# Twelve expert tiles set into the drain of a time-mix pipeline

## The chip, the cores and the metric

The kernel runs on one core of a Trainium2 chip. The metric is the device time of one execution in microseconds (us), lower is better; where several executions were timed, the median is given.

## What is computed

`x` has 64 sequences of 32 tokens with 256 channels (2048 tokens), `ctx` 64 sequences of 257. All arithmetic is float32. Three blocks follow each other, each with its residual:

```
x = x + xattn(layernorm(x), ctx)          # cross attention with LoRA projections
x = x + attn(layernorm(x))                # RWKV: time-mix, then a mixture of 8 experts
x = x + ffn(layernorm(x))                 # shared GEGLU + one of 8 GEGLU experts
```

The middle block is the one that matters here:

```
x  = x + (r * wkv) @ Wo                   # time-mix: a scan over the 32 tokens of a sequence
ei = ln(x);  exx = shift(ei)              # the row of the token before, zero for the first
probs = softmax(ei @ router_w);  two experts a token, weights vals / vals.sum
xk = ei * mk[e] + exx * (1 - mk[e]);  xr = the same with mr[e]
k_e = square(relu(xk @ eWk[e]));  kv = k_e @ eWv[e]        # 256 -> 512 -> 256
moe = sum over the two experts of  w * sigmoid(xr @ eWr[e]) * kv
```

## The kernel before

The 2048 tokens are G = 16 chunks of 128. Five engines run instruction streams of their own (SyncE `sp` only issues DMAs), held together by counting semaphores; within an engine the order of the program is the order of execution.

**Attention and time-mix** (`mix_sync`, `mix_pool`, `mix_tensor`, `mix_scalar`, `mix_vector`) are one software pipeline of STEPS = 25 steps. At step s attention works on chunks s to s-2, the time-mix on chunks s-3 to s-6 (LAG = 3), the router on s-7 and s-8; at s-9 the chunk's tokens are written into the table `tab_e` with two indirect DMAs (`list_tokens`, L475), by expert and rank. From step 16 on no new chunk enters: the pipeline drains. At step s GpSimd also makes the normed rows of chunk s-7 (`normed`, L460 and L462, four buffers `ei`), and SyncE stores them into `rows_e` (`store_normed`): one store of 128 rows (L326) and four of 31 rows, shifted by one token, for the four sequences of a chunk (L329). A buffer of `ei` is written again only when the store four chunks back has landed.

At step 18 SyncE issues the expert weights: `eWk` (4 MB, L354), `eWr` (2 MB, L356), `eWv` (4 MB, L358) and the small `Wg` (L360), ahead of that step's `store_normed`. They all go through SyncE's one queue. They lie in `arena_a`, over the keys and values of the attention, and so need it finished (`dv_x1`).

After step 24 TensorE makes the totals per expert (`totals`, L689) and VectorE the `tile_map` (L1017 to L1035): for each of NT1 = 39 tiles of 128 tokens its expert (`expert1`) and its place in `tab_e` (`place1`).

**The expert loop** (`moe_*`) then runs over 39 tiles in MSTEPS = 41 steps. SyncE loads the 128 token numbers of a tile (`pick`, L1131, nine tiles ahead). GpSimd copies the expert's mixing factors (`mu_e`, L1171) and gathers the pairs of rows by an indirect DMA (L1172, three tiles ahead); before the first it waits for every store of normed rows and for the tile map. At step m TensorE transposes tile m (L1192), does the hidden matmuls (L1200) and the receptance (L1207) of tile m-1 and the down projection (L1215) of tile m-2. ScalarE copies the transposed half and the expert's weights (L1231, L1234), then relu and sigmoid (L1238, L1241). VectorE mixes (L1271, L1278), squares (L1285) and gates (L1290); SyncE stores the result to `rows_y` (L1146). Buffers have NM = 3 slots. The steps are written out for the first 6 and the last 2, and run as a hardware loop of three steps a trip between them (`sweep`). At step 4 VectorE computes `slot1`, the row of `rows_y` of each token's two results (`rows_of`, L1253 to L1262). The combine, the second router and the GEGLU stages follow.

## Time and profile before

| | |
|---|---|
| median of 3 runs | 1026.53 us (1026.32 to 1027.2) |
| profiled execution | 1027.74 us, span of its instructions 1026.0 us |
| TensorE busy | 892.7 us (87%) |
| VectorE, ScalarE, GpSimd busy | 420.8 (41%), 293.2 (29%), 309.4 us (30%) |
| granted TensorE clock, mean | 0.942 of full |
| DMA | 163.55 MB, mean 159 GB/s |

The profile's times are microseconds from the first instruction. PE is TensorE's matmuls, PEld its weight loads (they overlap), DVE VectorE, ACT ScalarE, POOL GpSimd, SP SyncE; a q behind the engine marks a DMA that it issues. L460 is line 460 of the kernel before. A timeline row gives start, duration, engine, line, operation, what is written and from what, how many, and in brackets the idle time before it and what ended that. Names are those of the buffers in memory: nearly everything of the mix and the expert loop is called `arena_a`, `arena_b` or `bank`.

### The profile page before, as it was taken

The page shows a single profiled execution, that of the slowest core. Times are in us where ns is not written, and L with a number is a line of the kernel's source. Part 1 is how long each engine was busy: PE and PEld are TensorE (multiplying, and loading weights), DVE is VectorE, ACT ScalarE, POOL GpSimd, SP SyncE. Part 2 cuts the span into 40 slices and gives each one's busy share as a digit, 9 for nine tenths or more (in the row PEclk, how much of TensorE's full clock was granted, in tenths as well). Part 3 has the DMA queues.
Part 4 walks back from the last instruction along what each step waited for, and adds up shares of the span by engine and source line. Part 5 has one row for each costly group of instructions (what it writes and reads, how often), then busy time and mean ns, then how long its engine had stood idle before and what let it go on. Part 6 is the DMA issues. An engine that isn't in the chain of part 4 may idle for free. (4 is left out here: it accounts for less than half of the span.)

```text
span 1026.0 us, 20031 instructions
## 1 busy us (share of the span) xinstructions
PE 892.7 (87%) x6725; PEld 810.2 (79%) x6726; DVE 420.8 (41%) x1145; ACT 293.2 (29%) x666; POOL 309.4 (30%) x545
## 2 busy tenths in 40 slices
PE   5799999999730299999994999996899999999994
PEld 4577787887630299999994999995799999999993
DVE  2346776767841165555552333336211111111113
ACT  1345555554420155455441111110011111111110
POOL 1832555655652333322213222221210010110005
PEclk8899999999965599999997999998999999999998
DMA  9844555520791232263222111110598988899715
GB/s 345 268 170 155 182 128 165 192 73 22 197 220 41 57 88 78 78 202 89 77 61 62 31 35 43 31 31 26 196 321 331 312 310 327 296 324 328 261 57 164
DMA packets 100354, 163.55 MB, mean 159 GB/s; under 512 B 12440, under 2 KB 78616, under 8 KB 98104
## 3 DMA queue, kind: packets, MB, share of 16 engines
q1 hardware_dynamic: 86960, 120.93, 36.3%
q0 software_dynamic: 7552, 19.56, 7.3%
q10 hardware_dynamic: 5776, 22.22, 5.5%
q8 instruction: 37, 0.61, 0.3%
q14 instruction: 29, 0.24, 0.1%
HBM read 146.08 MB, written 16.60 MB: 159 GB/s over the span
## 5 line engine op out<-in xcount | busy, mean ns | idle before, releaser
L1524 PEld LDWEIGHTS bank<-zT_f,we 128*128 128x128 f32 x1472 | 167.8, 192 | 2.1 <-ACT zT_f L1812 0.7
L1524 PE MATMUL bank<-zT_f,we 128*128 128x128 f32 x1472 | 168.3, 275 | 0.5 <-ACT zT_f L1812 0.5
L1541 DVE TENSOR_TENSOR hT_f<-bank,act_g 128x512 f32<-128x512 f32 x78 | 53.9, 692 | 228.4 <-PE bank L1524 208.7
L1533 ACT ACTIVATE act_g<-bank 128x512 f32<-128x512 f32 x78 | 46.6, 597 | 321.5 <-PE bank L1524 318.0
L1524 PE MATMUL bank<-zT_c,a_x 128*128 128x128 f32 x1024 | 121.6, 281 | 0.3 <-PEq L1354 0.3
L1524 PEld LDWEIGHTS bank<-zT_c,a_x 128*128 128x128 f32 x1024 | 119.4, 197 | 0.8 <-issue 0.7
L572 PE MATMUL bank<-arena_b,mixed_w 128*128 128x128 f32 x768 | 91.5, 276 | 0.0
L572 PEld LDWEIGHTS bank<-arena_b,mixed_w 128*128 128x128 f32 x768 | 89.2, 192 | 1.0 <-issue 0.4
L1548 PE MATMUL bank<-we,hT_f 128*128 128x256 f32 x368 | 83.2, 379 | 0.0
L1200 PE MATMUL bank<-arena_b 128*128 128x128 f32 x624 | 77.8, 279 | 0.3 <-DVE hT L1285 0.2
L1200 PEld LDWEIGHTS bank<-arena_b 128*128 128x128 f32 x624 | 74.4, 195 | 0.9 <-DVE arena_b L1278 0.5
L1548 PEld LDWEIGHTS bank<-we,hT_f 128*128 128x128 f32 x368 | 68.1, 190 | 8.3
L1215 PE MATMUL bank<-arena_a,hT 128*128 x312 | 73.8, 379 | 0.7 <-DVE arena_b L1290 0.7
L1215 PEld LDWEIGHTS bank<-arena_a,hT 128*128 128x128 f32 x312 | 59.2, 190 | 9.1 <-issue 1.1
L1548 PE MATMUL bank<-mixed_w,hT_f 128*128 128x256 f32 x256 | 59.9, 388 | 4.1 <-issue 3.4
L1753 POOL COPY pick_f<-table 128x1 uint32 (+1 forms) x23 | 4.2, 184 | 186.5 <-PE bank L1774 159.1
L1548 PEld LDWEIGHTS bank<-mixed_w,hT_f 128*128 128x128 f32 x256 | 48.6, 195 | 11.0 <-issue 3.8
L1192 PE MATMUL bank<-ident,arena_b 128*128 128x128 f32 x156 | 24.4, 281 | 31.5 <-DMA arena_b<-rows_e,pick 30.4
L1192 PEld LDWEIGHTS bank<-ident,arena_b 128*128 128x128 f32 x156 | 19.9, 144 | 35.6 <-issue 30.4
L1278 DVE SCALAR_TENSOR_TENSOR arena_b<-arena_b,mu_e 128x128 f32<-128x128 f32 x156 | 45.4, 353 | 6.3 <-issue 6.0
L1231 ACT ACTIVATE arena_b<-bank 128x256 f32<-128x256 f32 x39 | 15.0, 384 | 115.2 <-PE bank L1192 115.1
L1234 ACT ACTIVATE arena_b<-arena_a 128x1024 f32 x39 | 41.2, 1057 | 13.1 <-issue 13.1
(249 smaller groups left out, 1323.6 us busy)
## 6 DMA issues: line engine op xcount, KB each, us to landing
we<-in_W_dram SPq DMA_DIRECT2D x69, 1024.0 KB, 7.2
arena_a<-in_ctx_n_dram ACTq DMA_DIRECT2D x16, 1152.0 KB
arena_a<-in_ctx_t_dram SPq DMA_DIRECT2D x16, 1028.0 KB, 9.8
rows_y<-arena_b SPq DMA_DIRECT2D x39, 128.0 KB, 2.0
arena_a<-in_eWk_dram SPq DMA_DIRECT2D x1, 4096.0 KB, 21.2
arena_a<-in_eWv_dram SPq DMA_DIRECT2D x1, 4096.0 KB, 38.4
rows_f<-yr ACTq DMA_DIRECT2D x23, 128.0 KB, 6.1
rows_e<-arena_b SPq DMA_DIRECT2D x16, 128.0 KB
```

Of the source, the lines that this page charges most:

```text
L572: last = nc.tensor.matmul(of_seq(bank[:, m * P:(m + 1) * P]), mixed_w[:, i, k, h, m * P:(m + 1) * P], xn[n % 2][:, k, :, 1 - h:1 - h + S], ...
L1192: last = nc.tensor.transpose(bA[:, q * P:(q + 1) * P], pair[:, a.slot, q * P:(q + 1) * P], ident[:])
L1200: last = nc.tensor.matmul(bHh[:, f * P:(f + 1) * P], wk_e[:, b.slot, k * FK + f * P:k * FK + (f + 1) * P], xk[:, b.slot, k * P:(k + 1) * P ...
L1215: last = nc.tensor.matmul(bY[:, 0:D], hT[:, d.slot, f * P:(f + 1) * P], ewv_sb[:, e, f * D:(f + 1) * D], start=f == 0, stop=f == FKC - 1)
L1231: nc.scalar.activation(prevT[:, a.slot], bA[:, 0:KD * P], ACT.Copy).then_inc(m_ap, 1)
L1234: nc.scalar.activation(wk_e[:, a.slot], ewk_sb[:, e], ACT.Copy).then_inc(m_awk, 1)
L1278: last = nc.vector.scalar_tensor_tensor(o[:, a.slot, h], diffT[:, a.slot, h], mu_e[:, a.slot, i, k:k + 1], prevT[:, a.slot, h], ALU.mult, ...
L1524: last = nc.tensor.matmul(bank[half][:, f * P:(f + 1) * P], w12[:, i, k, col0:col0 + P], zT[:, k], start=k == 0, stop=k == KD - 1)
L1533: nc.scalar.activation(act_g[:, half], bU[half][:], ACT.Gelu).then_inc(self.ac_g, 1)
L1541: nc.vector.tensor_tensor(hT[:, parity, half * HH:(half + 1) * HH].rearrange("p f t -> p (f t)"), bG[half][:], act_g[:, half], ALU.mult).t ...
L1548: last = nc.tensor.matmul(bY[parity][:, 0:D], hT[:, parity, f], w3[:, f], start=f == 0, stop=f == HC - 1)
L1753: nc.gpsimd.tensor_copy(pick[:, s.slot], table2[:, bass.ds(s.n, 1)]).then_inc(picked, 1)
```

## The change

- **Two phases of tiles.** The first CUT = 10 chunks are routed on their own. When chunk 10 is ranked (step 18), TensorE also makes the totals of the ten chunks and VectorE a first tile map (`tile_map_a`) of the *full* tiles only; TA = 12 of them are taken (`taken_a`: how many of each expert). The second map, after step 24, covers the other 27 tiles. `slot1` needs to know for each token which phase it fell into (`row_numbers`, now about eighteen VectorE operations, at expert step 12).
- **The expert steps are set into the drain.** Expert step m runs at the end of mix step s = 20 + m on each engine; the steps 0 to 4 share mix steps 20 to 24, the rest follow. At the end of step 19 SyncE issues the picks of the twelve tiles and GpSimd gathers the first three, which waits for these picks.
- **Weights in five pieces**: at step 16 `eWk` of experts 0 to 5 and `eWr` of 0 to 5, at 17 `eWk` 6 to 7 and `eWv` 0 to 4, at 18 `eWv` 5 to 7 and `eWr` 6 to 7, each *behind* that step's `store_normed`. `eWr` moves into `xz`, whose first chunks are free early; `w_T` and `early` move to the end of `arena_a`.
- **Unrolled, fewer buffers, other queue**: all 42 expert steps are written out. Weight copy, mixed rows, hidden and sigmoid have two slots instead of three. ScalarE issues the stores to `rows_y`, a step later. The expert loop uses the banks bS, bWV, bQR and bVV.

The core of the diff:

```diff
+        CUT = 10
+        TA = 12
+        MOE_AT = G + LAG + 1
+        MSTEPS = NT1 + 3
...
+        def moe_pick(sp, tiles):
+            for n in tiles:
+                mapped(sp, n)
+                if n == 0:
+                    sp.wait_ge(po_tab_a, 2 * 16 * CUT)
+                if n == TA:
+                    sp.wait_ge(po_tab, 2 * 16 * (G - CUT))
+                at = sp.value_load(place1[0:1, n:n + 1], min_val=0, max_val=T_ROWS // P - 1)
+                sp.dma_start(pick[:, n], tab_e[bass.ds(at * P, P), :]).then_inc(picked_by(n)[0], 16)
+
+        def moe_pool(pool):
+            def gather(n):
+                mapped(pool, n)
+                if n in (0, TA):
+                    for i in range(EI):
+                        pool.wait_ge(ei_out[i], OUT_PER * len(range(i, G if n else CUT, EI)))
...
+                e = pool.value_load(expert1[0:1, n:n + 1], min_val=0, max_val=E - 1)
+                need(pool, m_dx, n - NM + 1)
+                pool.wait_ge(*picked_by(n))
+                nc.gpsimd.tensor_copy(mu_e[:, n % NM], cm_mu[:, :, e]).then_inc(m_mu, 1)
+                rows = rows_e[0:CUT * P, :] if n < TA else rows_e[:, :]
...
+            def step(m):
+                if m < NT1:
+                    copies(m)
+                if 0 <= m - 1 < NT1:
+                    units(m - 1)
+                if 0 <= m - 3 < NT1:
+                    store(m - 3)
...
+                if m == TA:
+                    row_numbers()
...
+                if g is not None:
+                    store_normed(g)
+                if s == G:
+                    sp.wait_ge(pe_s, G)
+                    load_k(0, 6, 2)
+                    load_r(0, 6, 0)
+                if s == G + 1:
+                    sp.wait_ge(dv_o, G)
+                    load_k(6, E, 3)
+                    load_v(0, 5, 3)
                 if s == G + 2:
                     sp.wait_ge(dv_x1, G)
-                    sp.dma_start(ewk_sb.rearrange("p e (k f) -> p e k f", k=KD),
-                                 eWk.rearrange("e (k p) f -> p e k f", p=P)).then_inc(ld_moe[0], 16)
...
+                    load_v(5, E, 4)
+                    load_r(6, E, 1)
+                if s == MOE_AT - 1:
+                    moe_pick(sp, range(TA))
+            sp.dma_start(r2_w[:], Wg.rearrange("(k p) e -> p k e", p=P)).then_inc(ld_s, 16)
+            moe_pick(sp, range(TA, NT1))
...
+                if s == MOE_AT - 1:
+                    for n in range(NM):
+                        gather(n)
+                if s >= MOE_AT:
+                    moe(s - MOE_AT)
+            for m in range(STEPS - MOE_AT, MSTEPS):
+                moe(m)
...
+                if h == CUT:
+                    tile_map_a()
```

## Rows read from the trace of the kernel before

**Rows 1.** Busy us of each engine by stretch; granted clock, DMA share, GB/s
```profile
300.00:320.00 20.00, 0.89 (x6) 0.66 (x5) 1.40 (x9) 1.46 (x2) 3.89 (x7) 0.50 0.47 110
...
360.00:380.00 20.00, 20.00 (x136) 18.56 (x135) 11.92 (x35) 9.99 (x19) 7.65 (x12) 1.00 0.29 82
```

**Rows 2.** Waits from 250 to 360 us: total, times, longest
```profile
POOL arena_b L460 <- DMA rows_e<-arena_b: 15.8, 1, 15.8
```

**Rows 3.** Timeline of SyncE's DMA issues, 247 to 350 us
```profile
247.81 1.53 SPq L329 DMA_DIRECT2D rows_e<-arena_b  x4
...
262.19 0.41 SPq L354 DMA_DIRECT2D arena_a<-in_eWk_dram  x1
...
283.31 17.88 SPq L360 DMA_DIRECT2D r_w<-in_Wg_dram  x1
...
333.81 4.29 SPq L329 DMA_DIRECT2D rows_e<-arena_b  x4
339.21 10.32 SPq L1131 DMA_DIRECT2D pick<-tab_e  x10
```

**Rows 4.** DMA: GB/s in 40 slices (300 to 345 us); KB, us to landing
```profile
GB/s 244 264 210 122 88 169 191 170 66 134 24 25 24 24 134 24 25 24 8 12 123 2 9 8 4 0 14 24 25 24 133 25 24 25 24 25 24 25 24 9
...
pick<-tab_e SPq DMA_DIRECT2D x10, 0.5 KB, 2.7
r_w<-in_Wg_dram SPq DMA_DIRECT2D x1, 8.0 KB, 26.8
```

**Rows 5.** Timeline, 295 to 350 us: a drain step, the tile map, the first gathers
```profile
295.84 0.22 POOL L447 TENSOR_SCALAR rs<-mv 128x1 f32<-128x1 f32 x1
...
297.13 0.60 ACT L797 ACTIVATE arena_b<-a_x,rs 128x256 f32<-128x256 f32 x1 [1.75 <-POOL rs L451]
...
299.49 1.02 PE L623 MATMUL bank<-r_wg,arena_b 128*128 128x8 f32 x4
...
319.85 0.29 DVE L1017 TENSOR_TENSOR arena_b<-bank,tile_lo 128x128 f32<-128x128 f32 x1 [1.95 <-PE bank L689]
...
323.24 0.20 DVE L1035 TENSOR_TENSOR place<-te_f,tb_f 128x39 int32<-128x39 f32 x1
...
345.82 0.19 POOL L1171 COPY mu_e<-late 128x4 f32 x1 [23.68 <-issue]
...
349.27 0.98 POOL L1172 DMA_INDIRECT arena_b<-rows_e,pick  x1 [0.16 <-issue]
```

**Rows 6.** Timeline of the expert loop, 353 to 544 us
```profile
353.53 3.66 PE L1200 MATMUL bank<-arena_b 128*128 128x128 f32 x16
...
367.96 0.60 PE L1192 MATMUL bank<-ident,arena_b 128*128 128x128 f32 x4
...
372.77 0.60 PE L1192 MATMUL bank<-ident,arena_b 128*128 128x128 f32 x4
...
512.87 1.95 PE L1200 MATMUL bank<-arena_b 128*128 128x128 f32 x16
...
514.15 1.14 DVE L1278 SCALAR_TENSOR_TENSOR arena_b<-arena_b,mu_e 128x128 f32<-128x128 f32 x4 [0.16 <-issue]
...
517.69 1.95 PE L1200 MATMUL bank<-arena_b 128*128 128x128 f32 x16
...
543.80 0.43 DVE L1290 TENSOR_TENSOR arena_b<-bank,arena_b 128x256 f32<-128x256 f32 x1 [2.29 <-PE bank L1215]
```

**Rows 7.** Timeline of VectorE at expert step 4: first and last of five
```profile
368.50 0.16 DVE L1253 TENSOR_TENSOR moved<-t_end,n_tiles 128x8 f32<-128x8 f32 x1
...
369.98 0.22 DVE L1262 SCALAR_TENSOR_TENSOR slot<-moved_k,listed 128x32 uint32<-128x32 f32 x1
```

**Rows 8.** As rows 1, in stretches of 4 us
```profile
284.00:288.00 4.00, 1.92 (x13) 1.24 (x11) 3.60 (x12) 0.90 (x3) 2.15 (x3) 1.00 1.29 216
288.00:292.00 4.00, 1.37 (x3) 1.18 (x4) 3.10 (x11) 0.27 (x1) 3.45 (x8) 0.58 0.80 232
...
356.00:360.00 4.00, 3.80 (x27) 3.44 (x26) 2.18 (x7) 2.21 (x4) 2.02 (x4) 0.88 0.42 120
```

More of the change, by code:

```diff
@@ L210, in perceiver_block @@
         in_a = Carve(arena_a, FLOATS_A)
-        w_T = in_a.take(4, KD, D)
+        kT = [in_a.take(BG, KD, KW) for _ in range(N3)]
+        ctx_sb = in_a.take(N3, BG * TC * D + D)
         early = in_a.take(EARLY)
@@ L214, in perceiver_block @@
         bv_b, bo_b = early[:, 4:4 + D], early[:, 4 + D:4 + 2 * D]
-        ctx_sb = in_a.take(N3, BG * TC * D + D)
-        kT = [in_a.take(BG, KD, KW) for _ in range(N3)]
         hn, v_own, o_nat = (in_a.take(2, D) for _ in range(3))
@@ new lines, in moe_tensor, with turned, hidden, receptance @@
+        def moe_tensor(pe):
+            def turned(n):
+                pe.wait_ge(m_got[n % NM], n // NM * 16 + 16)
+                if n == 0:
+                    pe.wait_ge(ac_exp, G)
+                need(pe, m_dd, n)
+                for q in range(2 * KD):
+                    last = nc.tensor.transpose(bMT[:, q * P:(q + 1) * P], pair[:, n % NM, q * P:(q + 1) * P], ident[:])
+                last.then_inc(m_pa, 1)
+            def hidden(n):
+                pe.wait_ge(m_dx, n + 1)
+                pe.wait_ge(m_awk, n + 1)
+                if n == 0:
+                    pe.wait_ge(ac_er, G)
+                need(pe, m_dsq, n)
+                for f in range(FKC):
+                    for k in range(KD):
+                        last = nc.tensor.matmul(bMH[:, f * P:(f + 1) * P],
+                                                wk_e[:, n % 2, k * FK + f * P:k * FK + (f + 1) * P],
+                                                xk[:, n % 2, k * P:(k + 1) * P], start=k == 0, stop=k == KD - 1)
+                last.then_inc(m_ph, 1)
+            def receptance(n):
+                mapped(pe, n)
+                e = pe.value_load(expert1[0:1, n:n + 1], min_val=0, max_val=E - 1)
+                if n == 0:
+                    pe.wait_ge(dv_x1, G)
+                    pe.wait_ge(dv_v, G)
+                    pe.wait_ge(ld_moe[0], 16)
+                    pe.wait_ge(ld_moe[1], 16)
+                need(pe, m_asig, n)
+                for k in range(KD):
+                    last = nc.tensor.matmul(bMR[:, 0:D], xr[:, n % 2, k * P:(k + 1) * P],
+                                            ewr_sb[:, e, k * D:(k + 1) * D], start=k == 0, stop=k == KD - 1)
+                last.then_inc(m_pr, 1)
+            def down(n):
+                e = pe.value_load(expert1[0:1, n:n + 1], min_val=0, max_val=E - 1)
+                if n == 0:
+                    pe.wait_ge(dv_ev, G)
+                    pe.wait_ge(ld_moe[3], 16)
+                    pe.wait_ge(ld_moe[4], 16)
+                pe.wait_ge(m_dsq, n + 1)
+                need(pe, m_dy, n)
+                for f in range(FKC):
+                    last = nc.tensor.matmul(bMY[:, 0:D], hT[:, n % 2, f * P:(f + 1) * P],
+                                            ewv_sb[:, e, f * D:(f + 1) * D], start=f == 0, stop=f == FKC - 1)
+                last.then_inc(m_py, 1)
+            def step(m):
+                if m < NT1:
+                    turned(m)
+                if 0 <= m - 1 < NT1:
+                    hidden(m - 1)
+                    receptance(m - 1)
+                if 0 <= m - 2 < NT1:
+                    down(m - 2)
+            return step
@@ L730, in mix_tensor @@
                     router(g)
-            totals()
+                if s == STEPS - 1:
+                    totals()
+                if s >= MOE_AT:
+                    moe(s - MOE_AT)
+            for m in range(STEPS - MOE_AT, MSTEPS):
+                moe(m)
         def mix_scalar(act):
@@ L878, in mix_scalar @@
                     load_values(s + 2)
+                if s >= MOE_AT:
+                    moe(s - MOE_AT)
+            for m in range(STEPS - MOE_AT, MSTEPS):
+                moe(m)
         def mix_vector(dve):
@@ L1292, in perceiver_block @@
-        assert NT1 % NM == 0
+                if s == STEPS - 1:
+                    tile_map()
+                if s >= MOE_AT:
+                    moe(s - MOE_AT)
+            for m in range(STEPS - MOE_AT, MSTEPS):
+                moe(m)
         with nc.Block() as block:
```

430 lines of the change are left out of this document (232 added, 198 removed).

## The prediction, made before the change was run

> **What bounds the kernel now.** I read the table of 20 us stretches first. TensorE works 0.9 of the 20 us from 300 to 320, at the lower clock, and all 20 from 360 on [rows 1]; the hole begins near 288 and ends when the first gathered tile is there, near 350 [rows 8, 5]. It lies between the time-mix and the expert loop, and it is the only thing this change can fill. The list of waits of that stretch names a part: GpSimd waits 15.8 us for a store of normed rows [rows 2]. The queue of SyncE tells why. The three weight loads go out at 262.2 us, the queue is held until 283.31 + 17.88 = 301.2, and then the stores of chunks 11 to 15 fill it until 338.1; the first pick of a tile's tokens is issued at 339.2 [rows 3]. The small Wg load, queued behind the weights, lands at 283.31 + 26.8 = 310.1 us [rows 3, 4]; I take that as the end of the weights too. From then on it isn't bandwidth: the bandwidth row shows 24 GB/s between short peaks, which are the 31-row stores one after another (31 KB at 24 GB/s is 1.3 us) [rows 4].
>
> Inside the expert loop TensorE sets the pace: a tile follows a tile every 4.81 us with all 20 of 20 us busy [rows 1], and the chain transposes, ScalarE copy, VectorE mix ends 2.4 us before its matmuls begin (515.29 against 517.69) [rows 6]. So the loop's 39 tiles cost the same TensorE time after the change; what can change is when tile 5 begins (372.77 us now [rows 6]) and what interrupts the rest.
>
> **Sum, part one: when the first tokens are there.** The weights may go out behind the store of chunk 9, which is issued by 249.3 us, instead of at 262.2 [rows 3]: 12.9 us earlier. They took 47.9 us (262.2 to 310.1). Alone that gives 297 us. But the stores of chunks 10 and 11 are now inside this stream and that of chunk 12 ahead of the picks. Each is one 128-row store and four of 31 rows, 4.29 us of queue for the four [rows 3]; at 1.3 us each to move, and 0.8 for the large one, I take 6 us. Does such a store lengthen the stream or run beside it? Not shown by any row, so I bound it: nothing (297 us) or all of it, 2 x 6 (309 us). The row that is nearest is the 24 GB/s: under the weights the sixteen engines moved 216 to 232 GB/s together, 14 each [rows 8], so 24 is what a single one does alone, and the four stores follow each other as on one and the same engine. That engine's share of the weights then comes last, and a load is complete only with it. I take 309. Chunk 12's store, 6 us, makes it 315; the first pick, 2 us to land [rows 4], 317.
>
> The Trainium skill (DMA: Bandwidth & Descriptors, section on why a DMA increments its semaphore by 16) says that a copy uses the largest number of engines up to 16 that divides its slowest dimension, and the lowest-numbered ones, so 31 rows go to a single engine, always the same. It speaks against this change, and by it the stream ends at 309, not at 297. The rate of [rows 4] agrees with one engine; that it is always the same one no row shows.
>
> GpSimd now waits for these picks at the end of step 19, ahead of its share of steps 20 to 24. This is the wait that the change adds, and it replaces the 15.8 us at step 22 [rows 2]. Queued behind it are the reciprocal deviations, numerators, normed rows, counts and token lists of the last chunks; ScalarE, TensorE and VectorE wait for these. Three gathers take 345.82 to 350.25, 4.4 us [rows 5]. GpSimd is free for step 20 at about 317 + 4.4 = 321 us (bound below 297 + 2 + 4.4 = 303.5).
>
> **Part two: five drain steps with expert steps 0 to 4 in them.** Hand schedule from t0 = 321, durations of [rows 5, 6]; TensorE is at half clock at first. Step 20: three small GpSimd operations 1.3 (295.84 to 297.13), then normalise, transpose, copy, router 3.4 (297.13 to 299.49 + 1.02), transposes of tile 0 1.1, mix to t0 + 8.3. Step 21: GpSimd issues a gather behind that mix, 1.6, then 1.3 + 3.4 again, to 14.7; transposes 1.1, hidden at half clock 3.5, receptance 1.7, to 21.2. Step 22: ScalarE does the sigmoid first, then the same chain at full clock 2.7, then a whole tile of TensorE work 4.8 and the gate, 29.7. Step 23: four small VectorE operations and the ranks 1.5, 4.8 of TensorE and the gate 0.5, 36.6. Step 24: the tile map, 319.85 to 323.44 now with two operations more, 3.7; the difference 0.45 and then mixing to 42. TensorE could transpose tile 5 at 41.1 and is set back 0.4 by the mix: t0 + 41.5. So tile 5 begins at 321 + 41.5 = 362.5 us instead of 372.8: 10.3 us gained.
>
> The rest of the change, by its place: the first tile map (at VectorE's step 18) is some 13 small operations with drains, 3 us against the 3.6 of the present one; it delays GpSimd's step 19, which waits for the picks anyway: nothing, 3 us if that wait were gone. The extra totals matmul and its waits: nothing. Two buffers instead of three for mixed rows, hidden and weight copies: each is reused when the matmuls two tiles back are done, a whole step earlier than needed by the 4.81 us rhythm: nothing. Stores of y on ScalarE's queue, one a tile: a pick's issue is about 1 us of SyncE [rows 3], and a store's can't be dearer by its kind; ScalarE is busy 10 of 20 us in the loop [rows 1]: nothing. The 27 later picks: each about 1.03 us of SyncE (10.32 for ten [rows 3]), 28 us from the tile map at about 361; tile 12 is gathered four steps later and needs only the first; nothing. Shared weights: loaded at step 27 of the expert loop, 362 + 22 x 4.8 = 468 us, well before the loop ends.
>
> The row numbers at step 12 grow from five VectorE operations, 1.7 us [rows 7], to about eighteen with drains, 6 us. VectorE has 0.4 us idle there and the mix has the 2.4 us above: TensorE waits 6 - 0.4 - 2.4 = about 3 us, once (0 to 5). Unrolling: steps 4 and 5 are written out before too and lie 4.81 us apart (367.96, 372.77); inside the loop it is 4.82 (512.87, 517.69) [rows 6]: nothing. The Trainium skill (Runtime: NRT & Kernel Launch, Instruction fetch mechanics) holds that a taken branch can stall the fetch of instructions, which would make the unrolled loop faster; the equal distances show no such stall here.
>
> **Sum.** 10.3 - 3 = 7.3 us less. The profiled execution took 1027.7 us (span 1026.0), 1.2 above the median of 1026.5. 1027.7 - 7.3 = 1020.4 for it, **1019 us** as a median.
>
> **Rivals.**
> 1. *The small stores run beside the weights.* Then t0 is 303.5 and all else follows: 17.5 us more are gained, 1002 us. For it: the stores of chunks 10 and 11 are 0.3 MB of the stream's 10.8 MB. Against it: the 24 GB/s, and GpSimd's 15.8 us for a store that was queued behind weights [rows 2, 4].
> 2. *TensorE stays at 1.2 GHz.* The granted clock fell to 1.2 GHz within 288 to 292 us, after TensorE had been busy 1.9 of 4 us, and came back to 2.4 within 356 to 360 [rows 8], some 3 to 4 us after unbroken work had begun at 353.5 [rows 6]. I let it come back in step 22. If the gaps of the drain hold it down through steps 22 to 24, the 4.8 us of expert work are 9.6 in three steps: +14.4, and 1019 + 14 = 1033 us, slower than before. It decides from about two such steps on.
> 3. *It overlaps nothing.* The picks land so late (5 to 8 us later than I say, a slower stream, or the store of chunk 12 held longer) that the drain plus five tiles ends where the drain, the stores, the picks and five tiles ended before: t0 = 329 gives 1026 to 1027 us, no change.
>
> **Chances.** My forecast, with its errors of the store price, the clock by one step (+5) and the row numbers, 1012 to 1024: 0.54. Rival 1, whole or in part, 1000 to 1011: 0.22. Rival 3: 0.10. Rival 2 or another slower course: 0.14. A measurement of this kernel can tell about 0.2% (2 us) from no change. Faster 0.76, same 0.10, slower 0.14. The range takes in rival 1's bound and rival 3 and leaves out most of rival 2: 1001 to 1028.
>
> **What would show it.** Right: the first weight load at about 249 us; the first pick landing near 317 and GpSimd idle some 30 us before its first copy of mixing factors; TensorE's hole from about 288 to 320 only; tile 5's transposes near 362; one gap of TensorE of 3 us at step 12; 4.81 us a tile elsewhere; the last gate near 537 instead of 543.8. Wrong: the first pick near 300; half clock beyond the drain; gaps of TensorE in the steady steps (double buffers, fetch of instructions, ScalarE's stores); or GpSimd still waiting for a store at step 22.

## The result, and the profile after

The changed kernel takes 1014.99 us in the median of four executions (1010.54 to 1017.74), the kernel before on the same chip 1026.57 us (1026.32 to 1027.2). The ratio is 0.988, with a 95% interval of 0.985 to 0.992. The profiled execution took 1014.11 us with a span of 1012.3 us, 13.7 us less than the span before. The forecast was 1019 us with a range of 1001 to 1028. One execution of a later variant, the one with six picks on ScalarE's queue, ran at a mean granted clock of 0.82 instead of 0.95 and took 1094 us; the figures below leave it out.

The two stretches of 20 us that answer to [rows 1] show that there is still a hole between the time-mix and the expert loop. From 300 to 320 us TensorE works 4.9 us now and worked 0.9 before; in stretches of 4 us it does nothing at all from 288 to 312 us, and before it worked 0.4 us in all from 304 to 348. The columns are the same as there.

```profile
300.00:320.00 20.00, 4.89 (x18) 3.85 (x18) 1.50 (x6) 3.56 (x6) 8.93 (x15) 0.50 0.23 55
360.00:380.00 20.00, 20.00 (x134) 18.46 (x133) 10.72 (x28) 9.71 (x16) 4.75 (x9) 1.00 0.35 87
```

The list of waits from 250 to 360 us names the new cause. In place of the 15.8 us of [rows 2], GpSimd stands 24.6 us at the first copy of mixing factors, for a pick, and TensorE waits with it:

```profile
PE bank L842 <- ACT arena_b L1098: 35.3, 4, 28.3
...
POOL mu_e L358 <- DMA pick<-tab_e: 24.6, 1, 24.6
```

SyncE's queue, which answers to [rows 3], has the weights (L585, L589, L594) and the stores of normed rows (L579 the 128 rows, L582 the four times 31) one behind the other:

```profile
248.73 0.40 SPq L585 DMA_DIRECT2D arena_a<-in_eWk_dram  x1
...
259.52 6.14 SPq L579 DMA_DIRECT2D rows_e<-arena_b  x1
265.70 5.90 SPq L582 DMA_DIRECT2D rows_e<-arena_b  x4
...
291.15 3.85 SPq L594 DMA_DIRECT2D xz<-in_eWr_dram  x1
295.05 1.27 SPq L579 DMA_DIRECT2D rows_e<-arena_b  x1
296.36 5.00 SPq L582 DMA_DIRECT2D rows_e<-arena_b  x4
302.46 7.04 SPq L344 DMA_DIRECT2D pick<-tab_e  x7
```

The bandwidth from 250 to 310 us, in 40 slices of 1.5 us, answers to [rows 4]. The last piece of the weights lands 11.1 us after its issue, at 302.2 us. Three times the rate falls: to 24, 31 and 8 GB/s from 271 to 275.5 us, to 59, 42 and 40 from 287.5 to 292, and to 24 from 299.5 us for some eight us, each time behind one of the three groups of 31-row stores in the queue. In the last 2.7 us before the last piece of the weights lands nothing but that 24 GB/s moves.

```profile
GB/s 150 53 166 285 408 408 388 350 149 108 205 238 268 113 24 31 8 216 350 356 374 358 345 340 152 59 42 40 245 380 378 348 138 23 23 25 24 24 8 0
...
xz<-in_eWr_dram SPq DMA_DIRECT2D x1, 512.0 KB, 11.1
```

The timelines of GpSimd, TensorE and VectorE give the dates that the sum was built on: the first copy of mixing factors, GpSimd free for step 20, the transposes of tile 0, those of tile 5, and the last gate, the counterpart of 543.80 us in [rows 6].

```profile
308.13 0.18 POOL L358 COPY mu_e<-late 128x4 f32 x1 [24.62 <-DMA pick<-tab_e]
...
312.65 0.23 POOL L728 TENSOR_SCALAR rs<-mv 128x1 f32<-128x1 f32 x1
```

```profile
317.18 1.09 PE L397 MATMUL bank<-ident,arena_a 128*128 128x128 f32 x4
...
354.58 0.63 PE L397 MATMUL bank<-ident,arena_a 128*128 128x128 f32 x4
```

```profile
530.40 0.42 DVE L552 TENSOR_TENSOR arena_a<-bank,sig 128x256 f32<-128x256 f32 x1 [2.29 <-PE bank L436]
```

### The profile page after: what moved, and what is told of

The parts are those of the page before. It is cut to its first block and busy times, and to the rows that moved or that the text cites. A ratio compares the mean times of both kernels' runs of the same rounds, so it can differ in the third digit from the quotient of the medians.

```text
span 1012.3 us, 19824 instructions
## 1 busy us (share of the span) xinstructions
PE 898.9 (89%) x6726; PEld 815.5 (81%) x6726; DVE 424.4 (42%) x1173; ACT 294.3 (29%) x665; POOL 308.9 (31%) x547
## 5 line engine op out<-in xcount | busy, mean ns | idle before, releaser
L863 PE MATMUL bank<-arena_b,mixed_w 128*128 128x128 f32 x768 | 94.2, 281 | 0.0
L863 PEld LDWEIGHTS bank<-arena_b,mixed_w 128*128 128x128 f32 x768 | 91.9, 197 | 1.1 <-issue 0.4
L408 PE MATMUL bank<-arena_b,arena_a 128*128 128x128 f32 x624 | 79.1, 282 | 2.6 <-DVE hT L546 2.6
L408 PEld LDWEIGHTS bank<-arena_b,arena_a 128*128 128x128 f32 x624 | 75.8, 198 | 3.0 <-DVE arena_b L538 3.0
L1721 PEld LDWEIGHTS bank<-mixed_w,hT_f 128*128 128x128 f32 x256 | 49.7, 200 | 13.2 <-DVE hT_f L1714 6.5
L358 POOL COPY mu_e<-late 128x4 f32 x39 | 7.3, 187 | 126.1 <-DVE arena_b L538 101.4
L464 ACT ACTIVATE arena_a<-arena_a 128x1024 f32 x39 | 41.3, 1059 | 10.3 <-issue 10.3
L360 POOL DMA_INDIRECT arena_a<-rows_e,pick x39 | 38.3, 983 | 18.1 <-issue 18.1
L423 PE MATMUL bank<-xz,arena_b 128*128 x156 | 40.7, 384 | 0.0
```

Source lines behind the costliest of these rows:

```text
L360: nc.gpsimd.indirect_dma_start(out=pair[:, n % NM], out_offset=None, in_=rows, in_offset=bass.IndirectOffsetOnAxis(ap=pick[:, n], axis=0)) ...
L408: last = nc.tensor.matmul(bMH[:, f * P:(f + 1) * P], wk_e[:, n % 2, k * FK + f * P:k * FK + (f + 1) * P], xk[:, n % 2, k * P:(k + 1) * P], ...
L423: last = nc.tensor.matmul(bMR[:, 0:D], xr[:, n % 2, k * P:(k + 1) * P], ewr_sb[:, e, k * D:(k + 1) * D], start=k == 0, stop=k == KD - 1)
L464: nc.scalar.activation(wk_e[:, n % 2], ewk_sb[:, e], ACT.Copy).then_inc(m_awk, 1)
L863: last = nc.tensor.matmul(of_seq(bank[:, m * P:(m + 1) * P]), mixed_w[:, i, k, h, m * P:(m + 1) * P], xn[n % 2][:, k, :, 1 - h:1 - h + S], ...
L1721: last = nc.tensor.matmul(bY[parity][:, 0:D], hT[:, parity, f], w3[:, f], start=f == 0, stop=f == HC - 1)
```

## The experiments

Except for the changed kernel run again, which is the same to the letter, and the kernel before with split stores, every experiment carries one small difference beside its own: the fourth weight semaphore counts two loads in the changed kernel, and the experiments wait for both (`wait_ge(ld_moe[3], 32)`). No run takes that difference by itself. Times are medians; each is compared with the kernel before on the same chip (1027.7 to 1029.1 us in the four groups), and the ratio with its interval is what can be compared across groups.

| kernel | median, us | ratio, 95% | tile 5 transposes | last gate |
|---|---|---|---|---|
| changed kernel again | 1018.39 | 0.989 (0.987 to 0.992) | 355.4 | 534.0 |
| + split stores | 1008.67 | 0.982 (0.980 to 0.984) | 346.6 | 522.4 |
| + 3 picks on ScalarE's queue | 1005.82 | 0.978 (0.976 to 0.981) | 344.7 | 522.2 |
| + no expert step in the drain | 1020.28 | 0.993 (0.990 to 0.995) | 362.4 | 536.7 |
| + row numbers in three parts | 1011.67 | 0.983 (0.980 to 0.986) | 355.9 | 528.5 |
| kernel before + split stores | 1016.45 | 0.988 (0.985 to 0.991) | 359.2 | 530.3 |
| + 6 picks on ScalarE's queue | 999.28 | 0.973 (0.969 to 0.978) | 337.3 | 513.2 |
| all three: split, 6 picks, rows | 1000.12 | 0.972 (0.969 to 0.975) | 342.7 | 515.3 |
| 6 picks, rows | 994.59 | 0.969 (0.966 to 0.972) | 336.9 | 509.5 |
| all three, nothing in the drain | 996.76 | 0.969 (0.967 to 0.972) | 341.9 | 513.0 |
| 6 picks, rows, filler, too long | 997.30 | 0.970 (0.968 to 0.972) | 343.2 | 515.8 |
| 6 picks, rows, filler, fitted | 990.49 | 0.965 (0.963 to 0.967) | 333.5 | 506.1 |

The row of six picks has the median of three executions. The last two columns come from the profiled execution of each. Executions also differ ahead of the part that matters: the first weight load goes out at 246.9 to 250.3 us in the profiles of the variants with whole stores, which are the same up to there. So up to some 3 us of a difference between two rows of these columns can be that.

### The changed kernel again

> The changed kernel once more, on the same chip as the three variants beside it. Theory: span near 1012 us; the first pick lands near 308 us and GpSimd is free for mix step 20 near 312.6, because the picks lie behind the weights and the store of chunk 12 on SyncE's queue. If its time moves by some us from execution to execution (1010.5 to 1017.7 so far), the profile should show it in that landing or in the drain, not in the steady expert steps of 4.81 us.

It took 1018.39 us (1014.15 to 1019.02), as before within the spread. Its profile holds a find. Tile 5 comes 0.8 us later than in the first profile, but the last gate 3.6 us later. The timeline of TensorE shows where: after the pause at the row numbers (L397 waits 1.55 us, L408 1.29 us) the eight hidden matmuls (x16, since each float32 matmul is recorded twice) take 3.75 us.

```profile
401.99 0.63 PE L397 MATMUL bank<-ident,arena_a 128*128 128x128 f32 x4 [1.55 <-DVE arena_b L531]
403.90 3.75 PE L408 MATMUL bank<-arena_b,arena_a 128*128 128x128 f32 x16 [1.29 <-DVE hT L546]
...
411.17 0.60 PE L397 MATMUL bank<-ident,arena_a 128*128 128x128 f32 x4
```

In the first profile the same step ran with the same pause, but its matmuls took their 2.02 us:

```profile
401.17 0.63 PE L397 MATMUL bank<-ident,arena_a 128*128 128x128 f32 x4 [1.55 <-DVE arena_b L531]
403.08 2.02 PE L408 MATMUL bank<-arena_b,arena_a 128*128 128x128 f32 x16 [1.28 <-DVE hT L546]
...
407.53 0.60 PE L397 MATMUL bank<-ident,arena_a 128*128 128x128 f32 x4
```

The granted clock of the second look confirms it. From 404 to 408 us it was 0.50, that is 1.2 of the 2.4 GHz, right behind a stretch in which TensorE had been busy 1.16 of 4 us:

```profile
400.00:404.00 4.00, 1.16 (x8) 0.58 (x6) 3.51 (x12) 1.08 (x2) 0.19 (x2) 0.86 0.01 2
404.00:408.00 4.00, 4.00 (x18) 3.91 (x19) 2.31 (x6) 0.67 (x2) 2.66 (x4) 0.50 0.23 70
```

In the first profile the same 4 us behind the row numbers held as little work, 1.17 us, and the clock stayed:

```profile
399.20:403.20 4.00, 1.17 (x7) 0.59 (x7) 3.53 (x13) 1.10 (x2) 0.22 (x2) 1.00 0.00 1
```

With the lower clock the step took 9.18 us instead of 6.36. A pause of 3.3 us can cost another 2.8 us of clock, and whether it does differs between executions of one and the same kernel.

### Split stores in the changed kernel

```diff
-  OUT_PER = 16 * (1 + BG)
+  OUT_PER = 16 * (1 + 2 * BG)
...
-  sp.dma_start(rows_e[r + 1:r + S, 0:D], ei[j*S:j*S + S - 1, n % EI]).then_inc(ei_out[n % EI], 16)
+  for lo, hi in ((0, 16), (16, S - 1)):
+      sp.dma_start(rows_e[r + 1 + lo:r + 1 + hi, 0:D],
+                   ei[j*S + lo:j*S + hi, n % EI]).then_inc(ei_out[n % EI], 16)
```

> One change to the changed kernel: each store of 31 shifted rows is issued as 16 rows and 15 rows, for all chunks; nothing else (this and the other variants also wait for both loads on the fourth weight semaphore). Theory A (the 31-row stores all use one DMA engine, lengthen the weight stream from 47.9 to 53.5 us and hold the picks by another 5 to 6 us): the weights land near 297 instead of 302, the first pick near 299.5 instead of 308.1, the whole is about 8 us faster than the changed kernel, 1005 to 1008 us. Theory B (small stores cost a fixed time each, whatever engines they use): eight small stores a chunk instead of four, first pick at 308 or later, 1015 or more.

1008.67 us, 9.7 less than the changed kernel. The first weight load went out at 250.80 us, 2.1 us later, because eight issues take longer than four (3.59 us against 1.53). All weights had landed at 285.01 + 12.9 = 297.9 us. That is a stream of 47.1 us, as long as the 47.9 of the kernel before, against 302.2 - 248.7 = 53.5 with whole stores. The bandwidth over the same 60 us (250 to 310) no longer stays at 24 GB/s anywhere. The stream with the stores of chunk 12 in it ends near 298 us, falling from full rate to nothing without a stretch at 24 (368, 299, 103 GB/s, then 3), and the 189 behind it are the gathers:

```profile
GB/s 36 89 233 273 365 408 391 367 225 172 167 189 266 205 35 250 175 338 382 327 267 340 329 166 31 78 132 235 340 368 299 103 3 0 1 189 189 153 1 1
```

GpSimd's wait for the pick fell from 24.6 to 16.8 us (first copy at 300.12 instead of 308.13). So four 31-row stores move at 24 GB/s and lengthen the stream and the way to the picks; the same rows as 16 and 15 show no such stretch. That 24 GB/s is one engine of sixteen can be read twice. The DMA share, the mean over the sixteen engines, is 0.08 where only these stores run, and one of sixteen is 0.06; and sixteen together reach 408 GB/s in the row above, 25.5 each.

```profile
300.00:304.00 4.00, 0.00 (x0) 0.00 (x0) 0.00 (x0) 0.00 (x0) 0.00 (x0) 0.50 0.08 24
```

That line is the changed kernel's. The Trainium skill (DMA: Bandwidth & Descriptors, section on why a DMA increments its semaphore by 16) gives the rule from which I had taken this: the largest number up to 16 that divides the slowest dimension is one for 31 rows and 16 or 15 for the halves. These runs agree with it; that it is always the same engine they don't show.

### Split stores in the kernel before

The same edit at L329 and of `OUT_PER`, and nothing of the change.

> The kernel before, with each store of 31 rows made as one of 16 and one of 15 rows, and nothing else: what the engine imbalance cost before the change. Theory (each 31-row store is moved by one DMA engine alone, 1.3 us each, and the stores of chunks 11 to 15 follow each other that way from 301 to 338 us, with the picks behind): GpSimd's wait of 15.8 us for a store shrinks to some 8 us, the last store leaves the queue at 320 to 325 us, bounded by the issue of 45 descriptors at 0.42 us behind the weights, the picks go at 323 instead of 339, and tile 5 begins 12 to 17 us earlier: 1010 to 1015 us. That would be as much as the whole change brings. Rival (the cost lies in the number of stores or in their completions one by one): the tail stays until 335 or later, since there are nearly twice as many stores, and the time stays within 4 us or rises.

1016.45 us (1015.0 to 1017.89): the ratio, 0.988, is that of the whole change. The expected 1010 to 1015 was a little too good. In the queue of SyncE the last chunks follow each other every 4.0 us, nine issues at 0.4 us each, where those of the kernel before went out at 301.2, 309.4, 314.5, 320.1 and 332.6, 5 to 12 us apart:

```profile
305.52 4.79 SPq L330 DMA_DIRECT2D rows_e<-arena_b  x8
...
322.89 3.57 SPq L330 DMA_DIRECT2D rows_e<-arena_b  x8
329.52 10.71 SPq L1133 DMA_DIRECT2D pick<-tab_e  x10
```

GpSimd's wait for a buffer shrank only from 15.8 to 13.2 us, not to 8: the queue issued the stores of that buffer only from 305 to 310, behind the weights. The picks go at 329.5 instead of 339.2 us, the first copy of mixing factors is at 332.6 instead of 345.8, and tile 5 at 359.2 instead of 372.8. An edit of four lines thus takes 13.6 us out of the same hole into which the change puts its two phases of tiles. On top of split stores the change still brings 0.988 to 0.982, 6 to 7 us.

### Three picks on ScalarE's queue

```diff
+  if s == MOE_AT - 1:
+      moe_pick(act, range(NM))          # in mix_scalar, the same step
...
-  moe_pick(sp, range(TA))
+  moe_pick(sp, range(NM, TA))
```

On either queue the first picks also wait for the first tile map and for the token lists of ten chunks.

> One change to the changed kernel: the picks of the first three tiles are issued by ScalarE on its own queue at the end of its step 19; the other nine stay where they are. Theory A (the wait that the change added, GpSimd for picks behind weights and stores, sets the end of the drain): the picks land near 289 us, GpSimd is free near 293 instead of 312.6, everything behind it moves by 19 us less what TensorE then waits for weights (they land at 302, needed for the receptance of tile 0 near 307, so little): about 996 us, 994 to 1000. Theory B (the wait is cover only: weights, clock or gathers are late next): the gain is 8 us or less, 1006 or more, with TensorE waiting for a load or the gather.

1005.82 us, 12.6 less than the changed kernel, not 19. The first copy of mixing factors comes at 292.97, 15 us earlier. But at the fourth tile GpSimd waits again, 9.3 us, since that tile's pick still stands behind weights and stores in SyncE's queue:

```profile
292.97 0.18 POOL L359 COPY mu_e<-late 128x4 f32 x1 [9.21 <-DMA pick<-tab_e]
...
312.92 0.18 POOL L359 COPY mu_e<-late 128x4 f32 x1 [9.30 <-DMA pick<-tab_e]
```

I had priced the first wait and not looked at who waits next in the same queue. This run is also the second with a lower clock behind the row numbers (1.7 us).

### Nothing in the drain

```diff
-  MOE_AT = G + LAG + 1
+  MOE_AT = STEPS
```

> One constant of the changed kernel: the expert steps start after mix step 24 instead of at step 20, so no expert step is set into the drain; the first twelve tiles, their early table and the early weights stay. Theory A (the overlap itself brings nothing, since GpSimd's wait stops the drain; what gains is that the tables and weights are early): the drain runs through without the 24.6 us wait and ends near 310 us, but the picks now lie behind the stores of chunks 13 to 15, near 324; transposes of tile 0 near 328, of tile 5 near 351, against 356 effectively in the changed kernel: 1009 to 1012 us, 2 to 6 us faster than the changed one. Theory B (setting the steps into the drain is what gains): tile 5 near 372 as in the kernel before, 1025 us.

1020.28 us, by the median 2 us slower than the changed kernel again, though the intervals overlap (0.990 to 0.995 against 0.987 to 0.992), with the tile map of ten chunks, early weights and all else kept. The miss is in the picks. The drain no longer waits for them, so the stores of chunks 13 to 15 get into the queue first (to 329.0 us) and the picks go at 330.1:

```profile
304.06 13.70 SPq L582 DMA_DIRECT2D rows_e<-arena_b  x4
...
324.73 4.29 SPq L582 DMA_DIRECT2D rows_e<-arena_b  x4
330.13 8.13 SPq L344 DMA_DIRECT2D pick<-tab_e  x8
```

Tile 5 begins at 362.4, 7.0 us later than with the overlap, but the last gate only 2.7 us later (the second look at the changed kernel lost 2.8 to its clock at the row numbers, and 1.5 behind tile 5). With the queue in the way this run couldn't price the overlap; the run further below does.

### Row numbers in three parts

`row_numbers` is cut at its three `spread`s and called at expert steps 12, 14 and 16.

```diff
-  if m == TA:
-      row_numbers()
+  if TA <= m < TA + 6 and (m - TA) % 2 == 0:
+      (rows_a, rows_b, rows_c)[(m - TA) // 2]()
```

> The changed kernel with its row numbers (about nineteen VectorE operations, 5.5 us in one piece at expert step 12) spread over steps 12, 14 and 16. Theory (the pause of TensorE at step 12 costs twice: 3.3 us of waiting in every execution, and in some executions the granted clock falls to 1.2 GHz for one window behind it, as in the second look at the changed kernel, where the step after took 9.2 us instead of 6.4): transposes 4.8 to 5.3 us apart through steps 12 to 17, no lower clock between 385 and 420 us, 3 to 6 us less than the changed kernel and less spread from execution to execution. Rival (only the waiting counts, and the spread of 7 us comes from elsewhere): 3 us less, with the same spread. Rival (each third still delays the mix): three pauses of about 1 us, nothing gained.

1011.67 us. By the ratios (0.983 against 0.989) that is 6 to 7 us less than the changed kernel again, and the four executions lie within 2.8 us, where those of the changed kernel spread over 4.9 and 7.2. From tile 6 on the transposes are 4.81 to 4.82 us apart, with no pause and no lower clock:

```profile
400.79 0.60 PE L397 MATMUL bank<-ident,arena_a 128*128 128x128 f32 x4
405.61 0.60 PE L397 MATMUL bank<-ident,arena_a 128*128 128x128 f32 x4
```

That fits 3.3 us of waiting in every execution and up to 2.8 of clock in some. In how many isn't known: of the six profiled executions with the pause in one piece, two show the clock fall (9.18 and 8.01 us for the step instead of 6.36). Whether the lower clock explains the rest of the gain and the smaller spread, four executions of each can't settle.

### Six picks on ScalarE's queue

As the kernel with three, with `range(6)`.

> As the kernel with the picks of tiles 0 to 2 on ScalarE's queue, but the picks of tiles 0 to 5. Theory (there the wait moved to the fourth pick, which stood behind weights and stores in SyncE's queue, 9.3 us): no second wait of GpSimd, tile 5 at 297.5 + 42 = 339.5 us instead of 344.7, 1000 to 1002 us. Rival (what waits next is later by no more than 5 us: a buffer of normed rows whose store is still queued, or a piece of the weights for experts 6 and 7 that lands at 307): another wait takes its place and the time is within 2 us of 1006.

Ratio 0.973; the three executions took 997.97, 999.28 and 1003.96 us. The second wait is gone. Tile 5 begins at 337.3 (expected 339.5) and nothing takes the place of the second wait. The first is still there: GpSimd stands 9.4 us for its first pick, which ScalarE issues only at the end of its step 19.

### All three together, and without the split

> The three together in the changed kernel: 31-row stores in two parts, the picks of tiles 0 to 5 on ScalarE's queue, row numbers in three parts. Theory (three separate terms; with the picks out of SyncE's queue the split stores only free the buffers of normed rows and the weights earlier, so they add little): tile 5 at about 339 us, no pause at step 12, the last gate near 512, 995 to 999 us. If the split stores still add their 8 us on top, 988 to 992. Rival (ScalarE's queue and the shorter rhythm collide with the arrival of the weights, which land at about 298 us at the earliest, while the first expert matmuls come at 305): TensorE waits for weights in steps 21 and 22 and the time stays at 1000 or above.

1000.12 us, worse than the 995 to 999 expected, and no better than with the picks alone (0.972 against 0.973). So I took the split out again:

> The changed kernel with the picks of tiles 0 to 5 on ScalarE's queue and the row numbers in three parts, but the 31-row stores left whole. Theory (the kernel with all three was held up by the split itself: eight issues instead of four put the weights 2 us later and the picks landed a microsecond later beside them, while nothing waits for the split stores any more): tile 5 at 337 to 340 us, no pause at step 12, the last gate near 511, 995 to 997 us, 3 to 5 less than with all three. Rival (the kernel with the picks alone had an early front in its profiled execution by chance, 1.6 us): 999 to 1000 us, as with all three.

994.59 us. Without the split the median is 5.5 us lower, but the ratios, 0.969 and 0.972, lie in each other's intervals, so that it is faster isn't certain. What the runs do show is that the split brings no gain here. In the profiles tile 5 comes at 336.9 without it and at 342.7 with it; with it the weights go out at 250.5 instead of 247.1 us and the six picks on ScalarE's queue at 287.5 instead of 284.6. Of the 3.4 us between the weights some 2 are the four more issues of a chunk, as in the first split run; the rest is ahead of the edit. An edit worth 9.7 us while the picks waited behind these stores brings nothing once the first six don't.

### What the overlap itself is worth

The kernel with all three, with `MOE_AT = STEPS`: the picks of the first six tiles go out behind step 24 and the expert steps begin there.

> The kernel with all three (split stores, picks of tiles 0 to 5 on ScalarE's queue, row numbers in three parts), but with no expert step inside the drain: the twelve tiles are mapped and picked early, the picks are issued behind step 24, and the expert steps begin there. It shows what the overlap itself is worth once the queue is out of the way. Theory A (the drain, without GpSimd's wait, ends at about 309 us; the picks need 4 to 6 us, three gathers 4.4, then six tiles at 4.8: the first transposes at 319, tile 5 at 343): as with the overlap, tile 5 at 342.7, so the overlap by itself is worth nothing, 999 to 1002 us. Theory B (the overlap hides about five tiles of TensorE work, 20 us): 1010 us or more. Rival: the stores of chunks 13 to 15 and the clock, low after the hole, push it to 1005.

996.76 us, against 1000.12 with the overlap; the ratios, 0.969 and 0.972, lie in each other's intervals. Tile 5 begins at 341.9 without it and at 342.7 with it, and the last gate at 513.0 and 515.3, since without the overlap the 1.5 us pause behind the second tile map falls away. Theory B, a total that is some 20 us better by the overlap, is out. The timelines show why. First without expert steps in the drain (GpSimd's first small operation of steps 20, 21 and 22, then the transposes of tiles 0 and 5), then with them:

```profile
283.52 0.23 POOL L735 TENSOR_SCALAR rs<-mv 128x1 f32<-128x1 f32 x1
...
293.65 0.30 POOL L735 TENSOR_SCALAR rs<-mv 128x1 f32<-128x1 f32 x1
...
299.12 0.22 POOL L735 TENSOR_SCALAR rs<-mv 128x1 f32<-128x1 f32 x1
...
319.83 1.11 PE L398 MATMUL bank<-ident,arena_a 128*128 128x128 f32 x4 [12.51 <-DMA arena_a<-rows_e,pick]
...
341.94 0.60 PE L398 MATMUL bank<-ident,arena_a 128*128 128x128 f32 x4
```

```profile
295.06 0.18 POOL L359 COPY mu_e<-late 128x4 f32 x1 [12.01 <-DMA pick<-tab_e]
...
299.58 0.23 POOL L735 TENSOR_SCALAR rs<-mv 128x1 f32<-128x1 f32 x1
...
309.85 0.23 POOL L735 TENSOR_SCALAR rs<-mv 128x1 f32<-128x1 f32 x1
...
319.57 0.23 POOL L735 TENSOR_SCALAR rs<-mv 128x1 f32<-128x1 f32 x1
...
342.71 0.63 PE L398 MATMUL bank<-ident,arena_a 128*128 128x128 f32 x4
```

From GpSimd's step 20 to tile 5 it is 58.4 us without the overlap and 43.1 with it, 15.3 us less. But that step 20 begins 16.1 us later with the overlap, because GpSimd first waits 12.0 us for the picks and then issues three gathers. The two cancel. So the overlap does cover something: without it some ten us pass between the end of the drain on GpSimd (309.5) and the first gathered tile (319.83). About four more of the 15 are a wait of GpSimd for VectorE that falls away (below). All of it is paid for by the wait that the overlap puts ahead of the drain.

The shared steps themselves hide little. Steps 21 and 22 begin 5.5 us apart without an expert step, as in the kernel before (290.36 and 295.84), and 9.7 with one: 4.2 us more, for a tile that takes 4.81 us in the loop. (Steps 20 and 21 begin 10.3 us apart with the overlap, but they are no fair pair. Without an expert step they are 10.1 us apart, since GpSimd stands 3.9 us there for VectorE's time-mix, which in the other kernel is done during the wait for the picks.) A part of the length is the lower clock: in the last kernel of the next section these steps take 8.4 us. In the shared steps 20 to 23 GpSimd waits 2.3 to 2.9 us for VectorE's mix before it may gather the next tile, and only behind that gather begins the next chunk.

An overlap whose picks don't keep GpSimd waiting, with the gathers behind the operations of step 20, say, was not run. What the overlap could be worth stays open; what it is worth as it is set here is nothing.

### What the lower clock costs in the drain

Matmuls whose result nobody reads, into the bank that the next transposes overwrite, ahead of the first transposes of steps 20 to 22 of the 994.59 us kernel:

```diff
-  pe.wait_ge(ac_z3, n + 1)
   need(pe, ac_zT, n)
   upto(ac_xn, pe, n + 5)
+  for _ in range({13: 25, 14: 13, 15: 7}.get(n, 0)):
+      nc.tensor.matmul(bT[:, 0:D], ident[:], t_wo[:, 0], start=True, stop=True)
+  pe.wait_ge(ac_z3, n + 1)
```

The first try had 40, 14 and 0.

> The same kernel with TensorE kept busy in the two idle stretches of the drain: 40 matmuls whose results nobody reads ahead of the first transposes of step 20, some 10 us, and 14 ahead of those of step 21, some 3.4 us, while it would wait there for GpSimd and ScalarE. It measures what the lower clock costs in steps 20 to 22. Theory (the granted clock stays at 2.4 GHz, and the chains of normalise, transposes, router, tile transposes and hidden matmuls run at the durations of the later steps: 1.2 us in step 20, 2 to 3 in step 21, 1.6 in step 22): tile 5 some 5 us earlier, 990 to 992 us. Rival (other work hides TensorE's half speed there, since GpSimd and VectorE set the length of a drain step): the clock is full and the time is unchanged within 1 us. Rival (the clock falls all the same, the matmuls then take 20 us and hold up the first transposes): 8 us slower or more.

997.30 us. I had taken such a matmul for 0.24 us. One takes 0.436 (the trace records each float32 matmul twice, and I had counted records), so the 40 ran for 17.4 us and the transposes of step 20 stood 4 us behind them:

```profile
287.49 17.43 PE L846 MATMUL bank<-t_wo,ident 128*128 128x256 f32 x80
304.76 0.38 PE L849 MATMUL bank<-ident,arena_b 128*128 128x128 f32 x2
```

Another 3 us of the later tile 5 in this profile are not theirs: its first weight load was at 250.3 us, against 247.1 without the filler.

> The kernel with extra TensorE work in the drain again, with the counts set by the first try: there one such matmul took 0.436 us at full clock (17.43 us for 40, not 10), so the first transposes of step 20 stood 4 us behind them. Now 25 (10.9 us, in a gap of 12.4), 13 (5.7, in a gap of 6.4) and 7 ahead of step 22 (3.1, in a gap of 3.5, where the clock fell last time). Theory (the lower clock costs about 1 us in each of three drain steps, the rest of it hidden behind GpSimd, ScalarE and VectorE: the one undisturbed step went from 10.3 to 9.4 us): granted clock 1.00 from 284 to 340 us, tile 5 at the issue of the picks + 49.5 us instead of + 52.3, 991 to 993 us. Rival (the clock costs nothing that isn't given back by another engine in the next step): 994.6 within 1 us. Rival (half clock is paid in full: 4.8 us for each of steps 21 and 22): 985 to 988 us.

990.49 us (989.08 to 994.49). The granted clock is 1.00 in all of the 4 us stretches from 284 to 340. Two of them, first of the kernel without the filler, then with it:

```profile
288.00:292.00 4.00, 0.00 (x0) 0.00 (x0) 1.21 (x2) 0.00 (x0) 0.99 (x2) 0.50 0.55 136
...
308.00:312.00 4.00, 3.59 (x17) 3.59 (x18) 1.50 (x5) 1.32 (x4) 2.40 (x4) 0.50 0.13 22
```

```profile
288.00:292.00 4.00, 4.00 (x20) 3.54 (x19) 2.76 (x5) 0.00 (x0) 0.55 (x2) 1.00 0.46 138
...
308.00:312.00 4.00, 4.00 (x31) 3.85 (x32) 1.97 (x6) 2.39 (x5) 2.28 (x5) 1.00 0.12 20
```

From the first copy of mixing factors to tile 5 it now takes 42.6 us (290.91 to 333.54) instead of 46.5 (290.47 to 336.94). Half clock costs 3.8 us in the three drain steps: 0.9 in step 20, 1.3 in step 21 and 1.7 in step 22, the only one of them with a whole tile of TensorE work. That is more than the 1 a step of the theory and far less than TensorE's own doubled time. The times bear it out to within their noise (0.965 against 0.969, intervals that just overlap). Whether the kernel without the overlap would gain as much from such matmuls was not run. The Trainium skill (TensorE: Matmul & The Clock Gate, Part 1) says that the lower rate is the gate's default and activity releases it. That the activity may be useless is what these rows show. This kernel has the lowest time of the study, 3.5% below the kernel before.

## Why the prediction came out as it did

| step | predicted | measured |
|---|---|---|
| first weight load | 249.3 | 248.73 |
| weights complete | 309 (297 to 309) | 302.2 |
| first pick has landed | 317 | 308.1 |
| GpSimd free, t0 | 321 | 312.65 |
| tile 5 transposes | t0 + 41.5 = 362.5 | t0 + 41.9 = 354.58 |
| pause behind the second tile map | 0 | 1.5 |
| pause at the row numbers | 3 | 3.3 |
| last gate | about 537 | 530.40 |
| profiled execution | 1020.4 | 1014.11 |
| median | 1019 | 1014.99 |

**The price of the small stores was taken twice too high.** This is the step that was mis-sized. I added 2 x 6 us to the stream for the stores of chunks 10 and 11, the upper bound; they cost 53.5 - 47.9 = 5.6 us by the stream of before, and 53.5 - 47.1 = 6.4 by the run with split stores. The mechanism, that a 31-row store moves at the rate of one engine and holds up the stream, is shown by the two split runs, and rival 1 as a whole, that they run beside the weights for nothing, is out; in part it came true, since they cost about half of the upper bound. Why eight stores of 1.3 us add 6 and not 10.4 no run takes apart. The stream of before has low stretches of its own, as the middle of its bandwidth from 250 to 310 us shows, and in these a single engine's work may be hidden, which no run tests:

```profile
GB/s 9 8 18 24 19 0 11 89 44 120 94 156 402 392 408 395 309 217 141 188 241 367 369 285 154 94 158 384 358 264 195 129 130 228 261 165 104 171 186 94
```

The argument by which I chose the upper bound was right in its result and weak in its numbers: I set 24 GB/s against 14 an engine, the mean of a stretch that wasn't at full rate. At their best the weights move at 408 GB/s, 25.5 an engine.

The stores of chunk 12 and the landing of the pick took 5.9 us together (302.2 to 308.1) where I had 8. The three gathers took 4.5 (4.4 predicted). In all GpSimd was free 8.4 us earlier than I said.

**The hand schedule of the drain held**, 41.9 against 41.5 us, with the clock back a little later than I let it: the hidden matmuls of step 22 still ran at half clock (granted 0.57 from 336 to 340 us). That a later clock left the sum within 0.4 us is in part luck: the matmuls whose result nobody reads price a step at half clock at 0.9 to 1.7 us, so terms elsewhere in the schedule were about as much too dear, and no run says which. Rival 2 had a real cause and the wrong size: it charged 4.8 us for each step of TensorE at half clock.

**A pause of 1.5 us was missing.** The tile map grew by VectorE operations at step 24, and I let it delay only the mix. It also delays the squaring of the tile before: TensorE's hidden matmuls wait 1.27 us for `hT`, and the transposes behind tile 5 come 6.35 us later instead of 4.81.

**The row numbers** took 5.5 us on VectorE and cost TensorE 3.3 (predicted 3). Not foreseen is that this pause can bring the clock down. That may be a part of the change's larger spread.

**What cost nothing cost nothing.** The other steps of the expert loop are 4.81 to 4.82 us apart, as in [rows 6]: two buffers instead of three, the unrolled steps, ScalarE's stores and the 27 later picks don't show. These are readings of the profile; none of the four was undone by itself.

The sum closes. Tokens 8.4 us earlier, less 0.4, 1.5 and 0.3, is 6.1 us better than the 7.3 predicted: 13.4 = 543.80 - 530.40, and the span fell by 13.7. The forecast for the median was off by 4 us on the careful side. The other 2 of these 6 us are the choice of executions: the profiled one of the kernel before was 1.2 us above its median, that of the changed kernel 0.9 below. The sign was right, and so were the causes that the sum added up, but for one pause that it put at nothing.

What it did not see is larger than its error. I took the hole as something to be filled. The runs show that filling it brings nothing as it was done here (996.8 without, 1000.1 with expert steps in it), that 13.6 us of the hole in the kernel before were the price of 31-row stores in one queue, and that picks of 0.5 KB behind weights and stores were the next. I had named the wait for the picks at the end of step 19, and even counted it in, but took it as a date in the sum and not as the price of the overlap. Rival 3 has the right title, "it overlaps nothing", for the wrong reason: it let the picks land later than I forecast, and they landed 8.9 us earlier.

## What to carry to other kernels

Before moving work into a hole, ask what made the hole: here an edit of four lines to the store's shape in the kernel before was worth as much as the whole restructuring. Give what the critical path waits for a queue of its own, and then read that queue for the next one who waits, since the first fix only moved the wait to the fourth pick. Before setting work into another pipeline's steps, ask what that work has to wait for, since the pipeline then waits with it: here a wait of 12 us and three gathers ahead of step 20 took back the 15 us that were won behind it. And a step shared by two chains of small operations is not free because every engine in it has idle time: it grew by 4.2 us for a tile that takes 4.8 alone. An edit's worth has to be measured again after each other edit, as the split stores were worth 9.7 us at first and brought nothing at the end.

## What the runs showed of the hardware that I had not expected

- A pause of TensorE of 3.3 us in a stream of full activity brought the granted clock down in two of six profiled executions, and cost 2.8 us more in one and 1.7 in the other. The pause was the same in all six, and of two executions of one and the same kernel one kept its clock.
- TensorE does useless matmuls at a profit: 19.9 us of them in gaps took 3.8 us off the chain to tile 5 and 4 us off the median (0.965 against 0.969, intervals that just overlap).
- A 0.5 KB pick on a queue of its own still takes 4.2 to 6.7 us to land while the weights stream (4.2 with three picks, 5.7 with six, 6.7 with six and split stores), against 2.7 us for the picks in the kernel before, when the weights were in [rows 4].
- The trace records each float32 matmul twice, but a transpose once: 80 records of 17.43 us for 40 matmuls of 128x256, 0.436 us each, and x2 and x4 for the two and four transposes of a chunk and a tile. The x16 in 1.95 us of [rows 6] are eight matmuls.
